# Moving the softmax-weight normalisation from VectorE to GpSimd and the weight transposes to later places

## The reference, cut to what matters

```
q = l2norm(q) * qs;  k = l2norm(k) * ksc
q = q*cos*scale + rotate_half(q)*sin*scale      # k with 1/scale
sim  = einsum('bhwie,bhwje->bhwij', bq, bk2) * 8      # 32 x 64 per window
attn = softmax(where(mask, -max, sim), -1)
out  = einsum('bhwij,bhwje->bhwie', attn, bv2)
x = out @ Wo + x
x = a * gelu(gate) @ W2 + b2 + x      # after a layer norm and W1, 2 x 341 wide
```

## Time and profile before

| | |
|---|---|
| median of 3 runs | 3166.56 us |
| profiled execution | 3168.24 us, span 3166.5 us |
| TensorE | 3005.7 us busy, 95% |
| VectorE | 2880.3 us, 91% |
| ScalarE | 2272.7 us, 72% |
| GpSimd | 1807.9 us, 57% |
| TensorE's norms L806 waiting for GpSimd's L1287 | 4.1 us in all |
| VectorE's weight product L1377 | 192 x 1514 ns = 290.7 us |
| VectorE's transpose L1380 | 192 x 1246 ns = 239.1 us |
| TensorE clock granted | full in 0.99 of the span |

### The profile page before, as it was taken

One profiled execution on the slowest core, in us unless ns is written; L12 is line 12 of the kernel. 1 busy time (PEld: TensorE's weight loads), 2 busy tenths in 40 slices (PEclk: granted clock), 3 DMA queues, 4 the chain that ended last, 5 costly groups with the idle time before them and its releaser, 6 DMA issues.

```text
span 3166.5 us, 93664 instructions
## 1 busy us (share of the span) xinstructions
PE 3005.7 (95%) x37896; PEld 1857.5 (59%) x37896; DVE 2880.3 (91%) x2671; ACT 2272.7 (72%) x3707; POOL 1807.9 (57%) x823
## 2 busy tenths in 40 slices
PE   8699999999999999999999999999999999999996
PEld 4356555665665566565566656556656555665653
DVE  5599999999999999999999999999999999999995
ACT  4467777777777777776667777777777777777774
POOL 8556565555656555555445565555656565555652
PEclk9799999999999999999999999999999999999998
DMA  9544544543544544454344354454445445445542
GB/s 317 169 110 116 144 115 107 145 122 98 156 117 101 144 117 117 118 154 113 84 133 106 91 152 117 107 133 124 112 121 141 112 122 133 112 118 134 125 112 59
DMA packets 254405, 398.04 MB, mean 126 GB/s; under 512 B 51148, under 2 KB 84872, under 8 KB 254280
## 3 DMA queue, kind: packets, MB, share of 16 engines
q1 hardware_dynamic: 254280, 396.41, 47.8%
HBM read 64.64 MB, written 19.92 MB: 27 GB/s over the span
## 4 chain that ended last, share of the span: by engine, by line
PE 40%; DVE 23%; ACT 19%; issue 10%; SPq 1%; POOL 1%; DMA 1%; DVEq 0%; ACTq 0%; POOLq 0%
PE ps L848 6%; PE ps L806 5%; PE ps L866 5%; PE ps L882 5%; PE ps L827 5%; PE ps L787 4%; ACT f_ab L1094 4%; DVE f_mx L1362 4%; DVE f_p L1365 3%; ACT f_u L1093 3%; DVE f_p L1377 3%; ACT ps L1105 3%; PE ps L789 3%; PE ps L788 3%; ACT f_p L1111 3%
## 5 line engine op out<-in xcount | busy, mean ns | idle before, releaser
L1291 POOL TENSOR_TENSOR f_w<-f_w,f_ab 128x1024 f32<-128x1024 f32 x192 | 549.2, 2861 | 526.9 <-DVE f_w L1342 526.9
L1296 POOL TENSOR_TENSOR f_ab<-f_w,f_rn 128x1024 f32<-128x1024 f32 x192 | 594.1, 3094 | 390.9 <-DVE f_rn L1352 380.9
L1287 POOL TENSOR_TENSOR f_u<-f_u 128x512 f32<-128x512 f32 x384 | 589.1, 1549 | 365.3 <-ACT f_u L1093 359.8
L1094 ACT ACTIVATE f_ab<-ps,f_pa 128x512 f32<-128x512 f32 x768 | 542.1, 706 | 1.2
L1093 ACT ACTIVATE f_u<-ps 128x512 f32<-128x512 f32 x768 | 467.1, 608 | 99.3 <-PE ps L789 93.6
L1342 DVE TENSOR_TENSOR f_w<-f_ab,f_tan 128x1024 f32<-128x1024 f32 x384 | 500.4, 1343 | 4.1 <-POOL f_ab L1296 2.3
L848 PEld LDWEIGHTS ps<-f_tb,f_v 128*64 128x64 f32 x6144 | 396.0, 137 | 102.1 <-issue 78.5
L848 PE MATMUL ps<-f_tb,f_v 128*64 128x160 f32 (+1 forms) x6144 | 442.2, 297 | 11.9 <-DMA f_tb<-f_pt 10.7
L1105 ACT ACTIVATE ps<-ps 128x512 f32<-128x512 f32 x384 | 204.7, 574 | 340.7 <-PE ps L806 340.2
L787 PE MATMUL ps<-f_xh,f_wh 128*128 128x512 f32 x768 | 380.7, 496 | 54.8 <-ACT f_ab L1094 44.5
L806 PE MATMUL ps<-f_u,f_ones 128*128 128x512 f32 x768 | 370.2, 604 | 6.9 <-POOL f_u L1287 4.1
(11 more groups left out here) (165 smaller groups left out, 4822.9 us busy)
## 6 DMA issues: line engine op xcount, KB each, us to landing
f_kb<-f_ab SPq DMA_DIRECT2D x384, 256.0 KB, 3.6
f_qb<-f_ab SPq DMA_DIRECT2D x384, 256.0 KB, 3.6
f_tb<-f_pt SPq DMA_DIRECT2D x1344, 64.0 KB
f_wh<-split_w SPq DMA_DIRECT2D x48, 384.0 KB, 4.4
f_wl<-split_w SPq DMA_DIRECT2D x48, 384.0 KB, 4.2
a_w_raw<-wqkv SPq DMA_DIRECT2D x24, 384.0 KB, 4.6
split_w<-a_w_hi SPq DMA_DIRECT2D x24, 384.0 KB, 4.6
split_w<-a_w_lo SPq DMA_DIRECT2D x24, 384.0 KB, 5.5
```

The lines of the kernel that those rows point to most:

```text
L1094: nc.scalar.activation(ab[:, g % 2, i, :], bank("qk", g, i), ACT.Identity, scale=pa[:, g, i:i + 1]).then_inc(qk_read.sem, 1)
L1287: nc.gpsimd.tensor_tensor(u[:, 2 * i + 1, :], u[:, 2 * i, :], u[:, 2 * i + 1, :], ALU.add).then_inc(sq_sum[i].sem, 1)
L1291: nc.gpsimd.tensor_tensor(w[:, 0:2, :], w[:, 0:2, :], ab[:, k % 2, 0:2, :], ALU.add).then_inc(q_sum.sem, 1)
L1296: nc.gpsimd.tensor_tensor(ab[:, k % 2, 0:2, :], w[:, 0:2, :], rn[:, 0:1, :].broadcast_to([128, 2, N]), ALU.mult).then_inc(rope_q.sem, 1)
```

## The change

The product L1377 leaves VectorE's `turn_weights(g)` and becomes GpSimd's `normalise_weights(g)`. In GpSimd's list the product of quad 3 of the step before stands between the squares of quads 1 and 2, that of quad 0 behind the query normalisation of quad 1, that of quad 1 behind the query normalisation of quad 2, and that of quad 2 at the end. On VectorE, `turn_weights` is now the transpose alone, and it stands later: quad 3's after `add_keys(1)`, quad 0's after `turn(2)` (with `residual` now ahead of `turn(2)` directly), quad 1's after the three `gated`, and quad 2's in the next step after `turn(0)`. `POOL_USES` and `DVE_USES` list the register values that the steps keep ready; `g = -2` needs further ones. SP's, TensorE's and ScalarE's lists are unchanged.

```diff
                         if halves(s) != (None, None):
                             for k in range(3):
                                 add_squares(k)
                                 add_queries(k)
                                 normalise_queries(k)
+                                normalise_weights(k - 1)
                             add_queries(3)
                             add_squares(3)
                             normalise_queries(3)
+                            normalise_weights(2)
                         elif cur:
                             add_squares(0)
                             add_queries(0)
                             normalise_queries(0)
                             add_squares(1)
+                        if prev and halves(s) == (None, None):
+                            normalise_weights(-1)
+                        if cur and halves(s) == (None, None):
                             add_squares(2)
                             add_queries(1)
                             normalise_queries(1)
+                            normalise_weights(0)
                             add_queries(2)
                             normalise_queries(2)
+                            normalise_weights(1)
                             add_queries(3)
                             add_squares(3)
                             normalise_queries(3)
+                            normalise_weights(2)
...
+                        def normalise_weights(g):
+                            pool.wait_ge(p_inv.sem, now.count(p_inv, g))
+                            nc.gpsimd.tensor_tensor(pb, pb, rs[:, :].unsqueeze(1).unsqueeze(3).broadcast_to([128, 2, 16, WIN]), ALU.mult).then_inc(p_norm.sem, 1)
...
                         def turn_weights(g):
-                            dve.wait_ge(p_inv.sem, now.count(p_inv, g))
-                            nc.vector.tensor_tensor(pb, pb, rs[:, :].unsqueeze(1).unsqueeze(3).broadcast_to([128, 2, 16, WIN]), ALU.mult).then_inc(p_norm.sem, 1)
                             dve.wait_ge(p_norm.sem, now.count(p_norm, g))
                             dve.wait_ge(t_dma.sem, now.count(t_dma, g - 1))
                             nc.vector.transpose(pt[:, :], p[:, :]).then_inc(p_tr.sem, 1)
...
                         if cur:
                             turn(0)
+                        if prev:
+                            turn_weights(-2)
+                        if cur:
                             add_keys(0)
                             normalise_keys(0)
...
                         if cur:
                             turn(1)
+                            add_keys(1)
                         if prev:
                             turn_weights(-1)
                         if cur:
-                            add_keys(1)
                             normalise_keys(1)
                             less_maximum(0)
                             sums(0)
+                        if prev:
+                            residual()
+                        if cur:
+                            turn(2)
                             turn_weights(0)
-                        if prev:
-                            residual()
-                        if cur:
-                            turn(2)
                             add_keys(2)
...
                             sums(1)
                             evacuate_out()
-                            turn_weights(1)
                         if prev:
                             gated(0)
                             gated(1)
                             gated(2)
                         if cur:
+                            turn_weights(1)
                             next_low()
...
-                        if cur:
-                            turn_weights(2)
```

More of the change, by code:

```diff
@@ L493, in build_hybrid @@
                     *((16, c) for c in range(-15, 1)), (32, 32), *((128, c) for c in range(-96, 1, 32))]
-        POOL_USES = [*((4, c) for c in range(-3, 1)), *((8, c) for c in range(-6, 1, 2)), *((16, c) for c in range(-14, 1, 2))]
-        DVE_USES = [(1, -1), (1, 1), (3, -5), (3, -4), (3, -3), *((4, c) for c in range(-4, 2)), *((8, c) for c in range(-6, 1, 2)),
-                    *((16, c) for c in range(-12, 1, 4)), *((512, c) for c in range(-512, -127, 128))]
+        POOL_USES = [*((4, c) for c in range(-4, 1)), *((8, c) for c in range(-6, 1, 2)), *((16, c) for c in range(-14, 1, 2))]
+        DVE_USES = [(1, -1), (1, 1), (3, -5), (3, -4), (3, -3), *((4, c) for c in range(-5, 2)), *((8, c) for c in range(-6, 1, 2)),
+                    *((16, c) for c in range(-12, 1, 4)), *((512, c) for c in range(-640, -255, 128))]
         def stage_ffn():
@@ L1482, in step @@
                             sums(-1)
-                            turn_weights(-1)
                             turn(1)
                             ret_norm()
+                            turn_weights(-1)
                             add_keys(1)
@@ L1536, in step @@
                             sums(0)
-                            turn_weights(0)
                         if prev:
@@ L1541, in step @@
                             turn(2)
+                            turn_weights(0)
                             add_keys(2)
```

## The result

The changed kernel takes 3477.61 us (median of 4 runs, 3476.33 to 3479.62) against 3167.17 us for the kernel before (4 runs, 3165.83 to 3168.74). The ratio is 1.0981, with a 95% interval of 1.0962 to 1.1: 310 us slower, 6.5 us for each of the 48 steps. The prediction was 3470. The profiled execution took 3478.86 us; its mean granted TensorE clock was 0.977, before 0.990.

What follows compares the result with a forecast made beforehand. TensorE sets the step, with 1.8 us idle; VectorE's relief returns at most that. A + B + C = 6.4 us a step over 48 steps, +305 us, gives 3470 us; range 3270 to 3560.

Steps and rivals of the forecast that it cites:

- Rival 2: VectorE is the real limit, so the variance's square and the maximum come in time: 3128 us, or 3080; chance 0.06.
- rival 3: GpSimd's idle 25 us a step swallow the 9.4 us of products: no change, 3167 us; chance 0.03.
- Rival 1: TensorE waits only at norms(3); multiply costs 1.94 us or interplay is better: 1 to 3 us a step, 3270; chance 0.15.
- Chain A: Middle of the step: turn(2), moved transpose and GpSimd's queries delay centred, exponentials and hidden matmuls L882: +1.3 us.
- The product: The moved multiply on GpSimd, 1024 f32 elements with two inputs: taken as 2.35 us, at most 3.4.
- the prediction's own last line: Wrong if L806 waits no more than now, or if the multiply costs far from 2.35 us.
- lower by about 1.5 us a step: If the multiply follows L147's cheaper inner broadcast, the forecast sum falls by about 1.5 us a step.
- Chain B: Quad 1's product ahead of quad 3's queries and squares on GpSimd delays norms(3); with the middle-of-step delay, +3.3 us.
- the floor of 0.9 us: Quad 3's sums end some 0.9 us late for norms(3) even if VectorE came to turn(3) as early as possible.
- Chain C: Quad 2's product ahead of the next step's squares, which alternate with turn(0), makes norms(0) late: +3.1 us.
- What I cost at nothing: Quad 3's later transfers (0 to +1.4 us, taken as 0), other quads' transfers, the transpose's new position; retention-block steps at the same price.

Runs made afterwards that it cites:

- e10: Against the kernel before, only quad 3's product moved to GpSimd, the other products and all transposes left as they were: 3181.21 us, ratio 1.004.
- e2: GpSimd's list of the changed kernel with VectorE's list of the kernel before, each transpose at its old place: 3312.86 us, ratio 1.047.
- e9: The changed kernel with quad 2's transpose ahead of turn(0) instead of behind it: 3376.26 us, ratio 1.066.
- e7: The changed kernel with 4 extra TensorE matmuls, results overwritten, ahead of each half of norms(0): 3443.24 us, ratio 1.0866.
- e4: The changed kernel with GpSimd multiplying only 64 of 1024 weights a partition and filling 1500 scratch elements with zeros: 3408.66 us, ratio 1.0763.
- e1: VectorE's order of the changed kernel with the products kept on VectorE, and GpSimd's list of the kernel before: 3428.41 us, ratio 1.0824.
- e5: The changed kernel with quad 1's product behind add_squares(3) and add_keys(3) behind less_maximum(2), outside the retention-block steps: 3507.68 us, ratio 1.1078.

## Why the prediction was right, point by point

**What bounds the kernel.** Right. TensorE's idle time was all that VectorE could give back, and it gave back nothing: the wait L787 is unchanged, and L876 grew. Rival 2 (VectorE is the limit) and rival 3 (idle time swallows the products) fell; rival 3 holds for one product of the four, quad 3's in the steady steps (e10). Rival 1 shows a price that came true with a conclusion that did not: the product costs 1.91 us, but TensorE waits at `norms(0)` too. TensorE's share came to 89%, where 87% was forecast.

**Chain A, +1.3 us.** Right in place and size. L1135 starts at 842.76 and L882 at 843.66; less 6.16 these are 836.60 and 837.50, the numbers of the prediction. `centred` ends at 836.98, less 6.16 is 830.82, where 830.75 was worked out.

**The product.** Mis-sized. It takes 1.901 us at least and 1.912 in the median:

```profile
L1300 POOL TENSOR_TENSOR f_p<-f_p,f_rs x192: 1901/1912/2832, 147.3 to 3436.0; 128x1024 f32<-128x1024 f32 x192
```

I took 2.35, and the lower bound, 1.94 by L147's inner broadcast, was the one that held. By the prediction's own last line ("far from 2.35 us") this is a sign against it: the size of that term was wrong by a fifth, while the waits that it was to cause came. The rule of the "GPSIMD Engine Reference" in the Trainium skill, section 3.1, about 2.6 cycles an element for a body with two inputs, does not hold for this product: it takes 1.86 ns an element, and L1291 with two full operands 2.29. Nor does "lower by about 1.5 us a step" follow for the lower price: in the chains stand two products, 2 x 0.41 us, and 0.15 us of a third, 1.0 us in all. GpSimd's share came to 63%, and near 72% was forecast. That figure did not even follow from the prediction's own terms (1807.9 + 192 x 2.35 = 2259 us, of 3470 it is 65%); for no part of the rest does it give a term. The step's busy time grew by 43.76 - 35.83 = 7.9 us, which is little over the four products.

**Chain B.** Right mechanism, 1.1 us instead of 2.0. L812 starts at 856.93, less 6.16 is 850.77: A + B = 2.3 us, where 3.3 was forecast. The squares end at 853.27, less 6.16 is 847.1 instead of 847.9: 0.43 of that is the product, 0.2 the reciprocal (846.05 less 6.16 is 839.9 instead of 840.1) and the rest a shorter meeting with `next_low`. The last 0.2 us lie between the squares and the next step. That this place costs something even with VectorE's old order (the floor of 0.9 us) is borne out by e2, with 1.3.

**Chain C.** Right mechanism, 2.7 us instead of 3.1. The second half of `norms(0)` ends at 868.97, less 6.16 is 862.8, against 855.93 + 1.88 = 857.8 before: 5.0 us, less the 2.3 of A and B. The product and the alternating pair are where the prediction put them; the pair takes 4.45 us, where half turns and sums gave 4.65. By e9 and e7 the pair's alternation is 1.9 of the 2.7 us.

**What I cost at nothing.** Quad 3's late weights cost 0.8 us a step (`values(-1)` at 892.76 waits 0.81 for its transfers): inside the bounds of 0 to 1.4, but I had taken the 0. And "the new position of the transpose itself costs VectorE nothing more" is true of VectorE's time and misleading for the kernel's: e9 shows 101 us in the place of one transpose. "The five steps with the retention block ... get the same price" was wrong too: the six periods from `project_out(0)` of step 21 to that of step 27 take 443.6 us instead of 417.8, 4.3 us more each.

**The sum.** 1.3 + 1.1 + 2.7 + 0.8 = 5.9 us, of the 6.2 by which a step without a fallen clock is longer; 0.3 us is not assigned. With 4.3 us for the six periods around the retention block it makes 42 x 5.9 + 6 x 4.3 = 274 us. e7 measures 3443.24 - 3167.17 = 276 us with the clock kept, and the fallen clock, which the prediction did not foresee, adds 34: 310. So B and C were 1.3 us a step too dear, quad 3's weights 0.8 and the clock 34 / 48 = 0.7 too cheap. That 3470 came within 8 us of 3477.6 is in part luck, for these cancel; the 1.3 us alone would have been an error of some 60 us of 310.

**The rules on the engine choice.** VectorE lost 12 points of its share, and the kernel takes 9.8% longer. The Trainium skill's "Perfetto Trace Analysis", section "Optimizing Scalar/DVE Operations", gives the shared port as the reason to doubt such a move. The trace agrees in part: without most of the product's reading 69 of 310 us went (e4), and without the meeting of `turn(0)` and the square sums 101 (e9, 34 of them by the clock). The rest is the order in the two queues, which that warning does not speak of.

**Open.** How the 262 us of e1 divide over its three waits was read from the trace and not tested one by one. What makes the clock fall in some steps and not in others with the same waits was not tried. Nor was a kernel in which neither quad 1's nor quad 2's product stands ahead of squares and the transpose stands as in e9, so how far the whole loss can be taken back is not known.

## What to carry to other kernels

Before an instruction goes into another engine's in-order queue, look at what stands behind it there, when its inputs are ready, and how much slack its readers have on the engine that sets the end; the busy shares tell none of this. Test the order and the engine of such a change by themselves: here each alone cost less than both, their costs did not add up, and the one line that undid a third of the loss (e9) was found by seeing that a waiting VectorE kept GpSimd's sums undisturbed. Where a wait is removed in a loop of queues, look for the place to which it moves before counting it as a gain (e5). And before dividing a small loss by the number of steps, look in which steps it lies (e10).

## What the runs showed of the hardware that I had not expected

- A GpSimd product of 1024 f32 elements with an operand broadcast along the inner axis takes 1.91 us; with two full operands an add takes 2.34 us at least.
- Behind two waits of some 1.1 us close together (in one such step TensorE was busy 3.06 of 5 us) TensorE stood at 1.2 GHz for 3.4 us in 25 of the changed kernel's steps, and in others with the same waits it did not. Eight matmuls of 512 columns in these waits removed it, and 34 us with it. In e1 a fall of the same length stands ahead of another wait and costs nothing (66.4 us with and without).
- Two square sums of GpSimd, 2.49 us when VectorE stands at a semaphore, take 4.45 us beside two half turns of VectorE (4.04 us): at the shared interface the two engines went on by turns, instruction by instruction.
